# Routing tokens to tiles of one expert each, in place of computing every expert for every token

## The chip, the cores and the metric

The kernel runs on 1 core of one Trainium2 chip. The metric is the device time of one execution in microseconds (us); three runs of the kernel before gave a median of 170.99 us.

## The reference, cut to what matters

Eight batches of 128 tokens with 256 features go through a cross attention and then through a mixture of eight experts. The part that the change touches is the second:

```python
x = x + cross_attention(layernorm(x), ctx)
xf = layernorm(x).reshape(1024, 256)
probs = softmax(xf @ (gate_weight + 2 * gate_lora_B @ gate_lora_A).T)      # 8 experts
w, selected = top_k(probs, 2);  w = w / w.sum(-1)
gates, h = split(xf @ (gate_up[e] + 2 * lora), 2)                          # every expert e: 256 -> 2 x 128
out[e] = (silu(gates) * h) @ (down[e] + 2 * lora)                          # 128 -> 256
x = x + sum over the two selected experts of w * out[e]
```

## The kernel before, in words

P is 128 partitions, H 256 features, E 8 experts, I 128 hidden features, NT 8 batches. Each engine has its program written out by hand, with named counting semaphores between them, so each engine does its work in exactly the written order.

**Attention.** The loop over b in range(NT) (PE from L1123, ACT L448, DVE L709, POOL L298, SP L212) does for each batch the scores in both layouts (L908 for the maximum, L915 for the exponential), the row maximum on DVE (`max_chunk`, L593), its way to SBUF by a small DMA of SP (`load_max`, L205), the exponential on ACT (L391), the causal mask on POOL (`mask_chunk`, L295), the product with the values (`values`, L1024), the division (`softmax_divide`, L608 and L610), the output projection (`out_proj`, L998, by `products`, L798), the residual (L615), and the statistics of the second norm (L539, L540; `normaliser` on POOL, L253 to L259; `x2_normalise` on ACT, L420). `x2_T` (L1005) turns a normalised batch into features by tokens. In the same loop the low-rank parts of the expert weights are merged into `up_w` and `dn_w` (`lora_products`, `merge`, L586).

**Experts.** The merged weights are split into a high and a low fp32r part: the high part by ACT (`merge_high`), the low part by POOL (`merge_lows`, L286). Activations are split in the same way (`x2T_high`, `x2T_low`, `h_high`, `h_low`). The tokens form two groups of 512 (g = 0 and 1), and each of the 16 steps n (a group and an expert) computes one expert for all 512 tokens of a group: `gate_step` and `up_step` (six matmuls of 512 columns each, L798), silu on ACT (L410), `gate` on DVE (L664), the multiplication by the token's routing weight, zero where the expert wasn't chosen (`weigh`, L671), and `down_step` (12 matmuls of 256 columns, L1087), which sums over the experts in PSUM. Router logits are six matmuls of 512 columns per group; `route_choose` ranks them on DVE (L633 to L639). The weights reach all partitions over DRAM: SP writes them (L218) and loads eight broadcast copies of 256 KB per group (L226). `add_residual` (L654) adds the sum to `x_sb`, and SP stores two batches at a time (L231).

**Order around the change.** PE does `gate_step(0)` between the last attention block and `values(NT - 1)`; the last pieces of the attention are woven into the first expert steps. Four PSUM banks hold gate and up products of two steps, so PE works up to four steps ahead of `down_step`.

Of the kernel before, what the change touches and what calls it, by code (L numbers as in the profile page):

```python
# [12 lines left out]
def cross_attention_moe_kernel(nc, x, ctx_kv, Wq, Wkv, Wout, gate_w, gate_A, gate_B,  # L13
# [13 lines left out]
    NG = NT // GT  # L27
    GN = GT * P
# [12 lines left out]
    EXPERTS = (0, 4, 1, 5, 2, 6, 3, 7)  # L41
    HIGHS = (0, 4, 1, 5, 2, 3, 6, 8, 9, 7, 10, 11)
    HIGHS_AT = ((), (0,), (4, 1), (5,), (2,), (3,), (6,), (8,))
    LOWS_AT = (0, 1, 2, 1, 1, 1, 1, 1)
    UP_LOWS = (2, 2, 4, 4, 7, 7, 10, 10)
    DOWN_LOWS = (8, 8, 9, 9, 11, 11, 12, 12)

    ctx = ExitStack()
    with ctx:
# [18 lines left out]
        wr_hi = sb("wr_hi", [P, HC, P], F32R)  # L68
        wr_lo = sb("wr_lo", [P, HC, P], F32R)
# [7 lines left out]
        up_hi = sb("up_hi", [P, HC, E, 2 * I], F32R)  # L77
        dn_hi = sb("dn_hi", [P, E, H], F32R)
        up_lo = sb("up_lo", [P, HC, E, 2 * I], F32R)
        dn_lo = sb("dn_lo", [P, E, H], F32R)  # L80
        probsT = sb("probsT", [P, 2, NH, P])
        weight_all = probsT[:, :, :, :].rearrange("p k h n -> p (k h n)").rearrange("p (e n) -> p e n", e=E)
# [20 lines left out]
        x2hat = sb("x2hat", [P, H])  # L103
        lgT = sb("lgT", [E, GN])
        lg = sb("lg", [P, GT, E])
        lmax = sb("lmax", [P, GT])
        above = sb("above", [P, GT, E, E])
        equal = sb("equal", [P, GT, E, E])
        earlier = sb("earlier", [P, E, E])
        rank = sb("rank", [P, GT, E])  # L110
        chosen = sb("chosen", [P, GT, E])
        lsub = sb("lsub", [P, GT, E])
        lexp = sb("lexp", [P, GT, E])
        lpick = sb("lpick", [P, GT, E])
# [13 lines left out]
        xT_hi = sb("xT_hi", [P, HC, NT * P], F32R)  # L128
        xT_lo = sb("xT_lo", [P, HC, NT * P], F32R)
# [7 lines left out]
        silu = sb("silu", [P, 2, GN])  # L137
        gated = sb("gated", [P, 2, GN])
        h_f = sb("h_f", [P, 2, GN])
        h_hi = sb("h_hi", [P, 2, GN], F32R)  # L140
        h_lo = sb("h_lo", [P, 2, GN], F32R)
        rest_of_qk = sb("rest_of_qk", [P, 6 * GN])

        w_dram = nc.dram_tensor("weights", (NG, E, GN), F32, kind="Internal").ap()

# [9 lines left out]
        M_BANK = lambda b: bank[6][0:NH, PN:PN + P]  # L155
        X2_BANK = lambda t: bank[0 if t == GT - 1 else 5][:, 0:HC * P].rearrange("p (a n) -> p a n", a=HC)

# [11 lines left out]
        weight_loaded = [sem(f"weight_loaded{e}") for e in range(E)]  # L169
# [7 lines left out]
        xT_src = lambda g: slice(g * GN, (g + 1) * GN)  # L177
# [11 lines left out]
        def _(sp):  # L189
# [24 lines left out]

            for g in range(NG):

                sp.wait_ge(S_("wT_copied"), g + 1)
                sp.dma_start(w_dram[g], wT[:, g, :]).then_inc(S_("w_written"), 16)  # L218
                sp.wait_ge(S_("w_written"), 16 * (g + 1))
                for i in range(E):  # L220
                    if g == 0:
                        sp.wait_ge(S_("pv_done"), NT - 1 if i < E // 2 else NT)
                    else:
                        sp.wait_ge(S_("h_ready"), i + 1)
                    e = EXPERTS[i]
                    sp.dma_start(weight_all[:, i, :], w_dram[g, e:e + 1, :].to_broadcast([P, GN])).then_inc(weight_loaded[i], 16)  # L226
# [9 lines left out]
        def _(pool):  # L236
# [61 lines left out]
            for b in range(NT):  # L298
# [4 lines left out]
                if b >= 3 and b != GT + 2:  # L303
                    normaliser(1, b - 3, b - 2, "mv2_ready", b - 2)
# [941 lines left out]
```

## Time and profile before

| | |
|---|---|
| median of 3 runs (170.72 to 171.06) | 170.99 us |
| profiled execution: its own time, its span | 170.58 us, 168.8 us |
| PE busy | 153.3 us, 91% of the span |
| DVE, ACT, POOL busy | 105.4, 80.1, 53.5 us |
| chain that ended last: PE, DVE, DMA, ACT, issue | 65%, 14%, 8%, 5%, 5% |
| bytes moved by DMA | 11.18 MB |

The span runs from the first to the last instruction; the execution's own time holds 1.8 us more around it. "Busy" is the time in which an engine has an instruction under way; PE's matmuls overlap, so the duration of one is longer than the distance from one to the next, and what PE can do in a stretch is read from the distances. An fp32 matmul shows as two records. The chain follows back from the last instruction to what released each wait.

### The profile page before, as it was taken

The page shows a single profiled execution, that of the slowest core. Times are in us where ns is not written, and L with a number is a line of the kernel's source. Part 1 is how long each engine was busy: PE and PEld are TensorE (multiplying, and loading weights), DVE is VectorE, ACT ScalarE, POOL GpSimd, SP SyncE. Part 2 cuts the span into 40 slices and gives each one's busy share as a digit, 9 for nine tenths or more (in the row PEclk, how much of TensorE's full clock was granted, in tenths as well). Part 3 has the DMA queues.
Part 4 walks back from the last instruction along what each step waited for, and adds up shares of the span by engine and source line. Part 5 has one row for each costly group of instructions (what it writes and reads, how often), then busy time and mean ns, then how long its engine had stood idle before and what let it go on. Part 6 is the DMA issues. An engine that isn't in the chain of part 4 may idle for free.

```text
span 168.8 us, 3777 instructions
## 1 busy us (share of the span) xinstructions
PE 153.3 (91%) x1481; PEld 118.9 (70%) x1481; DVE 105.4 (62%) x224; ACT 80.1 (47%) x161; POOL 53.5 (32%) x93
## 2 busy tenths in 40 slices
PE   0597999999999999999999997999969989999972
PEld 0365676677777677778778876887758868888961
DVE  2778986859657657835498456555943466444463
ACT  1373557356657776586754617422653022222420
POOL 4276002256378657776740243330000000000000
PEclk9999999999999999999999999999999999999999
DMA  5999940000000000000000185000000594000003
GB/s 148 292 255 229 282 126 2 6 6 0 8 0 8 0 6 2 4 2 4 0 0 4 37 257 209 0 4 0 2 0 4 144 344 137 0 0 0 4 0 124
DMA packets 13042, 11.18 MB, mean 66 GB/s; under 512 B 6457, under 2 KB 10449, under 8 KB 13025
## 3 DMA queue, kind: packets, MB, share of 16 engines
q1 hardware_dynamic: 9584, 7.14, 15.7%
q0 software_dynamic: 544, 2.10, 4.6%
q10 hardware_dynamic: 2896, 1.70, 3.9%
q8 instruction: 12, 0.20, 0.5%
q14 instruction: 6, 0.04, 0.1%
HBM read 9.79 MB, written 1.08 MB: 64 GB/s over the span
## 4 chain that ended last, share of the span: by engine, by line
PE 65%; DVE 14%; DMA 8%; ACT 5%; issue 5%; POOL 1%; DVEq 0%; ACTq 0%
PE bank L798 29%; PE bank L1087 9%; PE bank L908 8%; DMA probsT<-weights 4%; PE bank L894 4%; PE bank L1024 4%; PE bank L915 3%; DVE m_sb L593 2%; DVE h_f L671 2%; DMA x_sb<-in_x 2%; DMA weights<-wT 2%; DVE xhat L552 2%; PE bank L973 2%; ACT silu L410 1%; DVE stats L539 1%
## 5 line engine op out<-in xcount | busy, mean ns | idle before, releaser
L798 PE MATMUL bank<-xT_hi,up_hi 128*128 128x512 f32 x64 | 27.1, 424 | 3.0 <-ACT silu L410 3.0
L318 ACT ACTIVATE h_hi<-h_f 128x512 fp32r<-128x512 f32 x16 | 10.1, 632 | 37.2 <-PE bank L1087 25.9
L295 POOL TENSOR_SCALAR_AFFINE_SELECT probsT<-probsT 128x512 f32<-128x512 f32 x32 | 19.7, 635 | 22.5 <-ACT probsT L391 22.5
L593 DVE TENSOR_REDUCE m_sb<-bank 128x4 f32<-128x512 f32 x32 | 20.4, 685 | 9.4 <-PE bank L908 9.4
L391 ACT ACTIVATE probsT<-bank 128x512 f32<-128x512 f32 x32 | 17.9, 590 | 17.3 <-PE bank L915 17.3
L798 PE MATMUL bank<-xT_hi,up_lo 128*128 128x512 f32 x64 | 25.3, 395 | 0.0
L798 PE MATMUL bank<-xT_lo,up_hi 128*128 128x512 f32 x64 | 25.3, 395 | 0.0
L676 DVE TENSOR_TENSOR h_lo<-h_f,h_hi 128x512 fp32r<-128x512 f32 x16 | 11.4, 713 | 21.0 <-ACT h_hi L318 21.0
L1087 PE MATMUL bank<-dn_hi,h_hi 128*128 128x256 f32 x64 | 18.4, 288 | 1.1 <-DVE h_lo L676 1.0
L915 PE MATMUL bank<-q_f,k_f 32*128 32x128 f32 x256 | 18.6, 283 | 0.0
L798 PEld LDWEIGHTS bank<-xT_hi,up_hi 128*128 128x128 f32 x64 | 12.0, 188 | 8.6 <-ACT silu L410 6.9
L1087 PE MATMUL bank<-dn_hi,h_lo 128*128 128x256 f32 x64 | 17.9, 279 | 0.0
L1087 PE MATMUL bank<-dn_lo,h_hi 128*128 128x256 f32 x64 | 17.8, 279 | 0.0
L908 PEld LDWEIGHTS bank<-k_f,q_f 32*128 32x128 f32 x256 | 13.6, 186 | 5.5 <-issue 5.0
L908 PE MATMUL bank<-k_f,q_f 32*128 32x128 f32 x256 | 16.3, 283 | 0.0
L915 PEld LDWEIGHTS bank<-q_f,k_f 32*128 32x128 f32 x256 | 15.5, 186 | 0.7 <-issue 0.7
L671 DVE TENSOR_TENSOR h_f<-probsT,gated 128x512 f32<-128x512 f32 x16 | 12.0, 748 | 5.1 <-DMA probsT<-weights 4.7
L798 PEld LDWEIGHTS bank<-xT_hi,up_lo 128*128 128x128 f32 x64 | 12.0, 188 | 2.9
L1087 PEld LDWEIGHTS bank<-dn_hi,h_hi 128*128 128x128 f32 x64 | 12.0, 187 | 2.1 <-DVE h_lo L676 1.5
L286 POOL TENSOR_TENSOR up_lo<-up_w,up_hi 128x512 fp32r<-128x512 f32 x8 | 10.3, 1291 | 9.8 <-ACT up_hi L318 9.8
L798 PEld LDWEIGHTS bank<-xT_lo,up_hi 128*128 128x128 f32 x64 | 12.1, 188 | 1.7
L1087 PEld LDWEIGHTS bank<-dn_lo,h_hi 128*128 128x128 f32 x64 | 12.0, 188 | 0.4
(137 smaller groups left out, 284.4 us busy)
## 6 DMA issues: line engine op xcount, KB each, us to landing
probsT<-weights SPq DMA_DIRECT2D x16, 256.0 KB, 5.5
x_sb<-in_x SPq DMA_DIRECT2D x4, 256.0 KB, 4.8
up_w<-in_L_ffn_gate_up_proj ACTq DMA_DIRECT2D x1, 1024.0 KB, 10.4
up_w<-in_L_ffn_gate_up_proj POOLq DMA_DIRECT2D x1, 1024.0 KB, 7.2
dn_w<-in_L_ffn_down_proj POOLq DMA_DIRECT2D x1, 1024.0 KB, 9.3
out<-x_sb SPq DMA_DIRECT2D x4, 256.0 KB, 2.2
ctx_sb<-in_ctx ACTq DMA_DIRECT2D x2, 128.0 KB, 5.6
wq_raw<-in_L_xattn_Wq ACTq DMA_DIRECT2D x1, 256.0 KB, 5.8
```

The costliest lines, as they stand in the source:

```text
L286: pool.tensor_tensor(merge_slice(up_lo, dn_lo, n), merge_slice(up_w, dn_w, n), merge_slice(up_hi, dn_hi, n).bitcast(F32), ALU.subtract).th ...
L295: pool.affine_select(out=ch, in_=ch, compare_op=ALU.is_ge, fill=0.0, base=0, pattern=[[0, 4], [1, P]], channel_multiplier=-1).then_inc(S_( ...
L318: act.activation(out_, in_, ACT.Copy, scale=scale).then_inc(S_(done), 1)
L391: act.activation(probsT[:, b % 2, 4 * j:4 * j + 4, :].rearrange("p h n -> p (h n)"), bank[2 + j % 2][:, :], ACT.Exp).then_inc(S_("exp_done ...
L593: dve.reduce_max(m_sb[:, b % 2, :].rearrange("p (u j t) -> p j u t", u=2, t=2)[:, c], S_BANK(b, c)[:, :].rearrange("p (u t n) -> p u t n", ...
L671: dve.tensor_tensor(h_f[:, k, :], weight_all[:, n % E, :], gated[:, k, :], ALU.mult).then_inc(S_("h_ready"), 1)
L676: dve.tensor_tensor(h_lo[:, k, :], h_f[:, k, :], h_hi[:, k, :].bitcast(F32), ALU.subtract)\
L798: last = pe.matmul(out_, a, m, start=start and i == 0, stop=stop and i == len(pairs) - 1, **kw)
L894: pe.matmul(S_BANK(s, j)[:, :], ident_b[:, :], causal[:, :, :].rearrange("p h n -> p (h n)"), start=True, stop=True, skip_group_check=True)
L908: last = pe.matmul(S_BANK(s, j)[:, c * P:(c + 1) * P], q_f[rows, c, tokens(s)], k_f[rows, c, tokens(s)], start=False, stop=True, skip_grou ...
L915: last = pe.matmul(bank[2 + j % 2][:, c * P:(c + 1) * P], k_f[rows, c, tokens(t)], q_f[rows, c, tokens(t)], start=True, stop=True)
L1087: last = pe.matmul(bank[6 + t // 2][:, (t % 2) * H:(t % 2 + 1) * H], a[:, k, tok], w[:, e, :], start=i == 0 and t % 2 == 0 and m == 0, sto ...
```

## The change

The expert part is rebuilt. The tokens form two groups of batches: batches 0 to 2 and 3 to 7. For every token DVE ranks the logits; a position for each (token, expert) chosen is counted by small matmuls with a triangle of ones; a token's row is written twice by indirect DMA of POOL to the rows of its two experts in a DRAM tensor that ACT has filled with zeros; SP loads tiles of 128 rows, each of one expert, at a row number read from a register. There are 13 tiles in the first group and 17 in the second, whatever the routing: the number that the worst case can need. For each tile PE transposes the rows, multiplies them in fp32 by the expert's weights, whose column PE reads into a register, transposes the hidden tile, and multiplies it by the down weights. The results of the first group are stored by SP to the same rows and gathered per token by indirect DMA of POOL; those of the second group are scattered by POOL to one row per (token, choice) and loaded back by SP. DVE adds the two rows of a token with their weights (`add_pair`). The split into high and low parts is gone.

```diff
+    ROUTED = ((0, 1, 2), (3, 4), (5, 6), (7,))
+    GROUP = (range(0, 3), range(3, NT))
+    ROWS = [len(g) * P for g in GROUP]
+    TILES = [(2 * n + E * (P - 1)) // P for n in ROWS]
+    SPARE = (7, 1)
+    XW = 272
+        xs = [nc.dram_tensor(f"xs{g}", (E * ROWS[g] + SPARE[g] * P, (H, XW)[g]), F32, kind="Internal").ap() for g in range(2)]
...
@@ SP
+            def load_tiles(g):
+                sp.wait_ge(S_("tiles_mapped"), g + 1)
+                sp.wait_ge(S_(f"x_scattered{g}"), 16 * 2 * len(GROUP[g]))
...
+                for i in range(TILES[g]):
+                    row = sp.value_load(row_x[g][0:1, i:i + 1], min_val=0, max_val=E * ROWS[g] + (SPARE[g] - 1) * P)
+                    sp.dma_start(xt[:, n, 0:(H, XW)[g]], xs[g][bass.ds(row, P), :]).then_inc(tile_loaded[n], 16)
...
+            load_tiles(0)
+            store_tiles(0, 5)
+            load_tiles(1)
+            store_tiles(5, TILES[0])
+            for b in GROUP[0]:
+                store_out(b)
+            sp.wait_ge(S_("y_scattered"), 16 * TILES[1])
...
+            for b in GROUP[1]:
+                sp.dma_start(yg[:, :, b, :], ys1[TILES[1] * P:, :].rearrange("(k j p) c -> j p k c", k=2, p=P)[j])\
+            for b in GROUP[1]:
+                store_out(b)
@@ POOL
+                if b == NT - 1:
+                    scatter_rows(0)
                 mask_chunk(b, 2)
                 mask_chunk(b, 3)
...
+            scatter_rows(1)
+            normaliser(1, 5, 6, "mv2_ready", 6)
+            scatter_rows(2)
+            normaliser(1, 6, 7, "mv2_ready", 7)
+            normaliser(1, 7, 8, "mv2_ready", 8)
+            for t in GROUP[1]:
+                scatter_rows(t)
+            for i in range(TILES[1]):
+                scatter_tile(TILE0[1] + i)
+                if 1 <= i < 4:
+                    gather_back(i - 1)
@@ ACT
+                if b == 0:
+                    fill(0, 0, E * len(GROUP[0]) + SPARE[0])
+                if b in (2, 4):
+                    half = E * len(GROUP[1]) // 2
+                    fill(1, *((0, half) if b == 2 else (half, 2 * half + 1)))
...
+            for s in range(NTILE):
...
+                    x_copy(s + 2)
+                    silu_step(s + 1)
+                    x2_again(4 + s)
+                    y_copy(s - 1)
+            y_copy(NTILE - 1)
+            exp_logits(3, NT, 2)
@@ DVE
                 if b == NT - 1:
-                    x2T_low(GT - 1)
+                    choose(0)
+                    slots(0)
+                    map_tiles(0)
                     residual(GT)
                     second_stats(GT)
...
+            for s in range(NTILE):
+                hT_copy(s)
+                    row_of_y(s)
+                    gate(s + 1)
+                if s == 0:
+                    choose(2)
+                if s == 1:
+                    slots(2)
+                if s == 3:
+                    choose(3)
+                if s == 4:
+                    slots(3)
+                    map_tiles(1)
...
+                if TILE0[1] + 5 <= s < TILE0[1] + 8:
+                    add_pair(s - TILE0[1] - 5)
+            pair_weights(3, NT, 2, len(ROUTED))
+            for b in GROUP[1]:
+                add_pair(b)
@@ PE
                 if b == NT - 1:
-                    router_logits(0, bank[1])
+                    positions(0)
...
+                if b == GT + 2:
+                    logits(0)
...
-            gate_step(0)
+            o_T_(NT - 2)
+            x2_T(4)
             values(NT - 1)
+            out_proj(NT - 2)
+            logits(1)
+            on_T(NT - 1)
+            tile_T(0)
+            x2_T(5)
             o_T_(NT - 1)
+            positions(1)
+            tile_T(1)
+            gate_up(0)
             out_proj(NT - 1)
+            x2_T(6)
+            for s in range(NTILE):
...
+                    tile_T(s + 2)
+                    gate_up(s + 1)
+                hidden_T(s)
+                    down_step(s - 1)
+                if last_of_group:
+                    down_step(s)
+                    tile_T(s + 1)
+                    tile_T(s + 2)
+                    gate_up(s + 1)
+            down_step(NTILE - 1)
```

The new functions that this calls, cut in the same way:

```python
def choose(r): # DVE: copy, is_gt, is_equal, mult, reduce_sum, is_lt, then one add per batch: 9 ops for ROUTED[0]
def slots(r): # DVE: mult, reduce_max, reduce_sum, subtract, minus one: 5 ops
def map_tiles(g): # DVE, on one partition: 12 ops
def pair_weights(lo, hi, nth, r): # DVE: 8 ops
def gate(n): h_f = bank[2 + n % 2][:, I:2 * I] * silu          # 128 x 128
def hT_copy(n): hT = bank[4][:, 0:P]                           # 128 x 128
def add_pair(b): two scalar_tensor_tensor of 128 x 256
def scatter_rows(t): # POOL: two indirect_dma_start of 128 rows
def gather_back(b): # POOL: two indirect_dma_start of 128 rows; the first waits for y_stored of all 13 tiles
def scatter_tile(n): # POOL: one indirect_dma_start of 128 rows
def logits(r): two matmuls x2T[:, t, ic, :], wr[:, ic, :] for each batch # 8 columns
def positions(r): two bf16 matmuls of 8 columns for each batch, one more at a group's end
def tile_T(n): two transposes of 128 x 128
def gate_up(n): value_load of the column; two fp32 matmuls 128 x 128 by 256 columns
def hidden_T(n): one transpose of 128 x 128
def down_step(n): one fp32 matmul 128 x 128 by 256 columns
def fill(g, lo, hi): act.dma_start(xs[g] rows lo * P to hi * P, zeros)
```

## Rows read from the trace of the kernel before

**Rows 1.** Stretches: start:end, length, busy PE PEld DVE ACT POOL, clock, DMA share, GB/s.

```profile
24.00:86.00 62.00, 61.08 (x927) 45.66 (x924) 41.81 (x95) 39.96 (x89) 35.86 (x57) 1.00 0.01 3
...
106.00:166.00 60.00, 56.34 (x327) 46.53 (x325) 32.94 (x57) 19.54 (x33) 2.58 (x2) 1.00 0.14 45
166.00:168.80 2.80, 0.00 (x0) 0.00 (x0) 0.22 (x1) 0.00 (x0) 0.00 (x0) 0.87 0.56 187
```

**Rows 2.** Chain that ended last: start us, us, what.

```profile
26.96 1.97 PE bank L798 x8
...
66.13 0.22 PE bank L984 x2
...
95.34 3.55 DMA probsT<-weights
...
142.33 1.41 PE bank L1087 x12
143.74 2.93 PE bank L798 x12
...
165.53 0.69 DVE x_sb L654
```

**Rows 3.** PE timeline around the last attention block: start us, us, then the operation.

```profile
76.72 1.16 PE L915 MATMUL bank<-q_f,k_f 32*128 32x128 f32 x16
```

**Rows 4.** DVE timeline, same stretch.

```profile
76.90 0.42 DVE L610 TENSOR_TENSOR o_nat<-bank,r_den 128x256 f32<-128x256 f32 x1
...
77.58 0.41 DVE L615 TENSOR_TENSOR x_sb<-bank,x_sb 128x256 f32<-128x256 f32 x1
78.03 0.43 DVE L539 BATCH_NORM_STATS2 stats<-x_sb 128x6 f32<-128x256 f32 x1
78.49 0.18 DVE L540 BATCH_NORM_AGGREGATE mv<-stats 128x2 f32<-128x6 f32 x1
```

**Rows 5.** POOL timeline, same stretch.

```profile
79.03 1.23 POOL L295 TENSOR_SCALAR_AFFINE_SELECT probsT<-probsT 128x512 f32<-128x512 f32 x2
80.34 0.22 POOL L253 TENSOR_SCALAR var_eps<-mv 128x1 f32<-128x1 f32 x1
80.64 0.56 POOL L254 TENSOR_TENSOR rstd<-var_eps,minus_half 128x1 f32<-128x1 f32 x1
81.30 0.27 POOL L259 TENSOR_SCALAR shift<-mv,rstd 128x1 f32<-128x1 f32 x1
...
86.07 0.30 POOL L253 TENSOR_SCALAR var_eps<-mv 128x1 f32<-128x1 f32 x1 [1.10 <-DVE mv L540]
86.45 0.73 POOL L254 TENSOR_TENSOR rstd<-var_eps,minus_half 128x1 f32<-128x1 f32 x1
87.29 0.51 POOL L259 TENSOR_SCALAR shift<-mv,rstd 128x1 f32<-128x1 f32 x1
```

**Rows 6.** Groups by line and form: busy us, mean ns, idle before.

```profile
L318 ACT ACTIVATE xT_hi<-bank 128x256 fp32r<-128x256 f32 x8 | 3.0, 380 | 3.0 <-PE bank L1005 3.0
...
L270 POOL DMA_DIRECT2D up_w<-in_L_ffn_gate_up_proj x1 | 1.1, 1110 | 0.0
...
L634 DVE TENSOR_TENSOR equal<-lg 128x256 f32<-128x256 f32 x2 | 0.9, 426 | 0.1
...
L624 DVE COPY lg<-bank 128x32 f32<-128x32 f32 x2 | 0.4, 192 | 4.3 <-PE bank L1036 4.3
```

**Rows 7.** ACT queue, issue of a 1 MB load.

```profile
2.94 0.54 ACTq L324 DMA_DIRECT2D up_w<-in_L_ffn_gate_up_proj  x1
```

**Rows 8.** SP queue, issue times.

```profile
4.35 3.81 SPq L194 DMA_DIRECT2D upB<-in_L_ffn_gup_lora_B  x1
...
95.34 4.38 SPq L226 DMA_DIRECT2D probsT<-weights  x8
```

**Rows 9.** DMA issues of the page: KB each, us from issue to landing.

```profile
probsT<-weights SPq DMA_DIRECT2D x16, 256.0 KB, 5.5
...
out<-x_sb SPq DMA_DIRECT2D x4, 256.0 KB, 2.2
```

More of the change, by code:

```diff
@@ new lines, in cross_attention_moe_kernel @@
+        full = [sb(f"full{g}", [1, E, len(GROUP[g])]) for g in range(2)]
+        iota_tile = sb("iota_tile", [1, max(TILES)], I32)
+        tile_no = sb("tile_no", [1, max(TILES)])
+        tile_row = sb("tile_row", [1, max(TILES)])
+        over = [sb(f"over{g}", [1, E, len(GROUP[g])]) for g in range(2)]
+        n_tiles = sb("n_tiles", [1, E])
+        part = sb("part", [1, E, E])
+        end = sb("end", [1, E])
+        skip = sb("skip", [1, E])
+        done = [sb(f"done{g}", [1, TILES[g], E]) for g in range(2)]
@@ L168, in cross_attention_moe_kernel @@
         m_loaded = [sem(f"m_loaded{i}") for i in range(2)]
[L169 removed]
+        tile_loaded = [sem(f"tile_loaded{n}") for n in range(NTILE)]
+        y_back = [sem(f"y_back{b}") for b in range(NT)]
         made = {}
@@ new lines, in positions @@
+            def positions(r):
+                pe.wait_ge(S_("chosen_ready"), r + 1)
+                if r == 0:
+                    pe.wait_ge(S_("router_consts"), 11)
+                for t in ROUTED[r]:
+                    g = group_of(t)
+                    j = t - GROUP[g][0]
+                    closes = t == GROUP[g][-1]
+                    products(slot_at(t), [(tri[:, :], chosen[:, t, :]), (ones[:, :], ahead[g][:, j, :])],
+                             "pos_ready" if t == ROUTED[r][-1] and not closes else None)
+                    if closes:
+                        products(count_at(g), [(ones[:, 0:1], ahead[g][:, j + 1, :])], "pos_ready")
@@ new lines, in tile_T @@
+            def tile_T(n):
+                pe.wait_ge(tile_loaded[n], 16)
+                if n == 0:
+                    pe.wait_ge(S_("x2T_copied"), GT)
+                elif n == TILE0[1] + 1:
+                    pe.wait_ge(S_("x1_ready"), NT)
+                elif n < TILE0[1] + 1:
+                    pe.wait_ge(S_("xt_copied"), n)
+                else:
+                    pe.wait_ge(S_("xt_copied"), n - 1)
+                for ic in range(HC):
+                    last = pe.transpose(XT_BANK(n)[:, ic, :], xt[:, n, ic * P:(ic + 1) * P], ident[:, :])
+                last.then_inc(S_("xt_T"), 1)
```

656 lines of the change are left out of this document (336 added, 320 removed).

## The prediction

> **What bounds the kernel now.** I read the stretches first. From 24 to 86 us (attention) PE is busy 61.08 of 62 us, from 106 to 166 us (the expert steps) 56.34 of 60, both at the full granted clock [rows 1]: PE sets the time in both, and only one real hole lies between them, where the broadcast weights come from DRAM, 3.55 us on the chain [rows 2]. Then the chain: an expert step is 2.93 us of gate and up products and 1.41 us of down products, 4.34 together [rows 2], so 16 steps are 69.4 us of PE. After the last matmul only two additions of 0.69 us [rows 2] and a store that lands 2.2 us after its issue [rows 9] are left, 168.8 us in all. The sum below is made on this clock; the execution's own time is 1.8 us more, 170.58, and that is 0.4 under the median of 170.99. The measurement can tell about 0.2% (0.3 us) from no change.
>
> **Expert work on PE: 69.4 us becomes 54.** Four fp32 matmuls of 128x128 by 256 columns take 1.97 us as eight records [rows 2], so 0.49 each. Two 128x128 transposes take 0.22 [rows 2], so 0.11 each. A tile has three such matmuls and three transposes: 1.47 + 0.33 = 1.80 us, and 30 tiles are 54.0. The routed tiles hold a quarter of the pairs and some padding, but such an fp32 matmul costs 0.49 against 1.41 / 12 = 0.12 for the same shape in fp32r [rows 2], so only 15 us are won. Steps overlap well in the written order: hidden_T(s) stands behind tile_T(s+2) and gate_up(s+1), 1.2 us, and what it waits for (a silu and a product of 128 columns, each under the 0.38 of a 256-column copy [rows 6]) is shorter. ACT has three operations of at most 0.38 per step, DVE two, so neither bounds. The two fp32r splittings go; they lay beside PE and give nothing by themselves.
>
> **The start of the first tile: a serial chain that the kernel before doesn't have.** Before, PE goes from attention straight into an expert step. Now a chain through DVE, POOL, DRAM and SP stands there.
> - logits(0), 12 records in block 6. Their distance isn't shown for 8 columns; bounds are nearly 0 and the 0.245 of a 256-column record; I take a transpose's 0.11, so 1.3 us. Block 7 then starts at 76.72 + 1.3 = 78.0 [rows 3].
> - DVE's division of block 5, before at 76.90 [rows 4], is done at about 78.5. choose(0) is nine operations between 0.19 (32 columns) and 0.43 (256 columns) [rows 6]: 2.5 us, to 81.0. PE's positions(0) waits for it, some 0.8 us. slots(0), five of 0.19, and map_tiles(0), twelve of 0.19 to 0.25 on one partition, follow: 3.7 us, to 84.7.
> - Residual(4) and its statistics, moved behind these, take 0.41 + 0.43 + 0.18 [rows 4]: 85.8. PE's out_proj(5) waits for this residual, and POOL's normaliser for the statistics: 0.22 + 0.56 + 0.27 [rows 5], to 86.9.
> - On POOL the first scatters stand behind this normaliser. An indirect issue isn't in the trace. Nearest are POOL's plain DMA issue, 1.11 us [rows 6], and as ends 0.2 (its smallest operation [rows 5]) and 3.81 (an issue of SP with many small pieces, on a full queue [rows 8]). I take 1.1. Two scatters, two masks (1.23 [rows 5]), two scatters, a normaliser (1.05), two scatters: 8.9 us, to 95.8. values(7) waits for the masks; PE has little else and idles for most of 88 to 101.
> - The rows land about 1.8 us later (2.2 less the issue of 0.4 [rows 9]), SP reads a register, issues (0.4) and the tile lands 2.2 after that: about 100.8.
> - PE then has tile_T(0), x2_T(5), o_T_(7), tile_T(1), gate_up(0), out_proj(7) and x2_T(6) with their copies: the loop begins at 104.2, where before steps 0 to 3 had their products nearly done.
>
> **The loop.** 54.0 less the two tile_T and the gate_up(0) already done (1.4) is 52.6. Beside the tiles PE has x2_T(7), logits and positions of five batches: 2.3. DVE's slots(3) and map_tiles(1), 4 us in one go before the next hT_copy, exceed its slack of about 2: 2.0. The group boundary, where down_step(12) waits for its copy and gate_up(13) for tile 13's: 1.1. A register read by PE before each gate_up isn't in the trace: below it is 0, since it may run while the products queued before it are at work; above, 0.54, a whole DMA issue of ACT [rows 7]. I take 0.1, near the low end, since 0.7 us of queued work lies ahead of it: 3.0. The Trainium skill ("DMA: Bandwidth & Descriptors", Latency and other measured facts) gives a floor of about 600 ns for such a load; all of it exposed would make this term 18 us. No row here shows one.
> The second group's loads start after slots(3), near 114, and the last scatters: about 119.5, and its first tile is wanted at 135, so they are hidden.
>
> **The fill.** ACT issues zeros for 31 and 41 blocks of 128 rows: 4.1 and 5.7 MB of writes, near 33, 47 and 61 us, where DMA moves 3 GB/s [rows 1]. Eight loads of 256 KB issued from 95.34 in 4.38 us [rows 8] with 5.5 us to landing [rows 9] make about 0.3 MB/us, so the writes end long before 95. What they can meet are the small loads of the maxima, and ACT's queue: an issue for four times the rows of the 1 MB load (0.54 [rows 7]) is some 2 us; with a full queue, as SP's 3.81 [rows 8], more. I take 1.0 on the path (0 to 13, the latter the whole first fill).
>
> **The tail.** After the last down_step: y_copy 0.5, indirect issue 1.1 and landing 1.8, five SP loads of 256 KB, the last issued 1.7 later and landing 5.5 after that, less overlap, 6.6 with the wait; add_pair of two 0.43 operations 0.9; store 2.2 and a hand-over: 13.2. pair_weights(3..7) is some 4 us and lies beside it. Before, this was 3.4.
>
> **Sum:** 104.2 + 1.0 + 52.6 + 2.3 + 2.0 + 1.1 + 3.0 + 13.2 = 179.4, plus 1.8 is 181.2. I forecast 181 us, 6% slower. Its own range, from terms other than the rivals', is 175 to 188.
>
> **A: faster.** Everything is dear because I priced each hand-over singly. If an indirect issue is 0.6 us, the chain is 3 us shorter (tile 0 at 98); with fill, register reads and DVE's hold all covered (6.0), and five loads at 0.3 MB/us from the first byte (tail 10.5): 181.2 - 3.0 - 6.0 - 2.7 = 169.5. For it speaks that 15 us of PE work truly go and that the lookahead is two tiles; against it that all must come at once, since the start chain is of DVE operations whose prices are shown. It decides if tile 0 is transposed before 98 and a step is 1.80. Chance 0.13; about level, 170.9: 0.02.
>
> **B: POOL becomes the bound.** In rows, the same three normaliser operations take 0.22, 0.56, 0.27 alone and 0.30, 0.73, 0.51 at 86 us [rows 5], beside DVE's comparisons: POOL is slowed by DVE, by half. In the second group POOL has 17 scatters and 6 gathers against 17 steps of 1.9 us; it decides from 32 / 23 = 1.4 us an issue. At 1.8 the start is 4 us later and POOL ends 41 us after the group's first tile (140 + 41 = 181), then the rest of the tail: about 195. The Trainium skill ("SBUF — State Buffer", Who interferes with whom) says that VectorE and GpSimd share a port pair under an exclusive lock, so the later of the two fully blocks, and that a GpSimd DMA can't write its descriptors while DVE is in a two-port mode. By that rule, the slowed rows agree. Chance 0.20.
>
> **C: SP's queue holds DVE.** SP does 17 loads, then 8 stores of first-group tiles, and only then may POOL gather; add_pair(0), in step 18, stands before the next hT_copy on DVE. With 0.75 us for register and issue, stores end near 140, in time. From 1.0 us on they are late; at 1.3 they land at 154, the gather at 158, and DVE waits 10 us from 147: 192. Against: the eight issues of 4.38 us are 0.55 each [rows 8], and the register read must then be dear. Chance 0.12.
>
> **D: the fill blocks ACT** for the length of a queue that is full (3.81 [rows 8]) or more, and exponentials wait: +8, 189. Chance 0.08.
>
> That leaves 0.45 for the forecast; slower altogether is 0.45 + 0.20 + 0.12 + 0.08 = 0.85. The range reaches from 168 (A and a little more) to 199 (B).
>
> **What would show it.** In the profile after: fp32 matmul records 0.245 us apart and steps of 1.9 us; PE idle from about 88 to 101, released by the DMA into xt; POOL's indirect issues near 1.1 us (B: 1.4 or more, and POOL on the chain at the end); SP's loads 0.75 apart (C: DVE's scalar_tensor_tensor released by DMA yg in the middle of group 1); ACT's fill issue near 2 us (D: above 4). In the hole PE may also lose its full clock, as it does after its last work (0.87 in the last 2.8 us [rows 1]): first tiles at the lower level would add up to 3 us. The prediction is wrong if the hole is under 5 us or the last tile ends before 155.

## The result, and the profile after

The kernel after takes 214.55 us (median of 4 runs, 212.0 to 218.45), the kernel before 171.03 beside it: ratio 1.2426, 95% interval 1.2351 to 1.2501. The medians and spreads given are over all executions of a kernel, but in kernels with the change some executions are slow ones, over 1.5% longer than the fastest, and every ratio, and every difference between kernels below, leaves these out (the kernel after is then 212.6). The forecast was 181 us with a range of 168 to 199. The sign was right (slower), the size was not: 41.5 us lost instead of 10, and no case of the range reached that far. The profiled execution took 212.0 us with a span of 210.2, so 30.8 us more than the span of 179.4 that the sum gave.

First the stretches of the kernel after, to hold against [rows 1]: start:end, length, busy PE PEld DVE ACT POOL, clock, DMA share, GB/s.

```profile
24.00:80.00 56.00, 52.98 (x797) 38.96 (x796) 34.85 (x73) 31.09 (x70) 22.50 (x42) 0.97 0.54 178
80.00:92.00 12.00, 10.42 (x94) 7.90 (x94) 8.24 (x33) 3.37 (x7) 1.65 (x4) 0.64 0.01 1
92.00:108.00 16.00, 7.75 (x59) 5.33 (x57) 5.92 (x21) 3.06 (x7) 10.29 (x16) 0.71 0.15 58
108.00:118.00 10.00, 7.33 (x29) 5.23 (x29) 2.17 (x10) 5.08 (x11) 1.30 (x4) 0.69 0.39 112
118.00:136.00 18.00, 13.98 (x77) 10.50 (x77) 10.37 (x51) 7.16 (x23) 9.70 (x10) 1.00 0.41 142
140.00:160.00 20.00, 18.41 (x92) 14.12 (x93) 5.69 (x27) 9.72 (x32) 1.94 (x2) 1.00 0.46 133
160.00:172.00 12.00, 2.38 (x13) 1.64 (x11) 0.43 (x1) 1.49 (x6) 3.83 (x4) 0.72 0.30 98
172.00:176.00 4.00, 2.90 (x9) 2.33 (x9) 1.49 (x6) 0.77 (x2) 3.08 (x4) 0.50 0.41 131
...
200.00:210.20 10.20, 0.00 (x0) 0.00 (x0) 4.94 (x12) 0.00 (x0) 0.00 (x0) 0.50 0.60 193
```

Three things differ from before. Attention moves 178 GB/s instead of 3 and PE is busy 95% of it, not 98.5%. The clock, at 1.00 before to the end of the experts, is 0.64 to 0.71 from 80 to 118 (and already 0.50 from 74 to 76). From 160 to 172 PE does almost nothing, and behind its last product, which ends at 196.6, stand 13.6 us where [rows 1] has 2.8.

The chain shows what ended last (start us, us, what); [rows 2] is its counterpart:

```profile
34.54 5.90 DMA q_f<-mT
...
66.39 5.63 DMA q_f<-mT
...
102.77 2.39 DMA xs<-xrow,index
106.21 2.04 DMA xt<-xs
...
164.70 1.69 DMA xs<-y_sb
168.62 2.85 DMA probsT<-xs,index
...
197.81 2.42 DMA ys<-y_sb,y_row
201.18 3.98 DMA probsT<-ys
```

Every hand-over through DRAM is on it, and two of the small loads of the maxima, 5.90 and 5.63 us long. PE's timeline names the waits in its brackets:

```profile
72.07 1.16 PE L1040 MATMUL bank<-q_f,k_f 32*128 32x128 f32 x16 [1.44 <-DMA q_f<-mT]
...
86.63 0.18 PE L923 MATMUL bank<-chosen,tri 128*128 128x8 bf16 x1 [1.39 <-DVE ahead L729]
...
108.29 0.69 PE L1197 MATMUL bank<-ident,xt 128*128 128x128 f32 x2 [5.60 <-DMA xt<-xs]
...
161.27 1.11 PE L923 MATMUL bank<-up_w,xh 128*128 x4
173.10 0.47 PE L1223 MATMUL bank<-ident,h_f 128*128 128x128 f32 x1 [10.72 <-DVE h_f L800]
...
174.70 1.91 PE L923 MATMUL bank<-up_w,xh 128*128 x4
177.08 0.48 PE L1223 MATMUL bank<-ident,h_f 128*128 128x128 f32 x1 [0.46 <-DVE h_f L800]
```

The wait of 10.72 us is released by DVE's gate. What DVE itself had waited for, and what POOL, stands in their timelines:

```profile
171.57 0.48 DVE L791 SCALAR_TENSOR_TENSOR x_sb<-probsT,wts,x_sb 128x256 f32<-128x256 f32 x1 [11.83 <-DMA probsT<-xs,index]
...
175.51 0.48 DVE L791 SCALAR_TENSOR_TENSOR x_sb<-probsT,wts,x_sb 128x256 f32<-128x256 f32 x1 [2.46 <-DMA probsT<-xs,index]
...
167.25 1.06 POOL L368 DMA_INDIRECT probsT<-xs,index  x1 [10.73 <-DMA xs<-y_sb]
```

And SP's queue, which POOL's gather waits for (start, length of the whole group, count):

```profile
106.21 14.99 SPq L254 DMA_DIRECT2D xt<-xs  x13
124.12 9.72 SPq L260 DMA_DIRECT2D xs<-y_sb  x5
137.20 18.72 SPq L254 DMA_DIRECT2D xt<-xs  x17
156.86 8.18 SPq L260 DMA_DIRECT2D xs<-y_sb  x8
```

This is rival C, complete: 17 loads of 1.1 us each, then 8 stores, the last at 165.0; POOL's gather at 167.25; DVE's sum of tile 0 at 171.57, with the next hT_copy behind it; PE stands. The forecast had these loads begin at 119.5; they began at 137.20, behind the last scatters (133.97, landing 2.44 later). When PE resumes, the clock is 0.50 and the four records of gate and up take 1.91 us instead of 1.11. But the clock doesn't pace the next two steps. They take 4.0 us each (hidden_T at 173.10, 177.08 and 181.12), because the gate that each waits for stands on DVE behind the sum of tile 1 (175.51) and that of tile 2 (179.59). These wait for POOL's next gathers, which come 4.0 us apart, two gathers and a scatter at a time. Kernels 2 and 4 show the same two steps of 4.0 us. They are still rival C.

### The profile page after: what moved, and what is told of

Read it like the earlier page. It is cut to its first block, busy times and chain, and to the rows that moved or that the text cites. A ratio compares the mean times of both kernels' runs of the same rounds, so it can differ in the third digit from the quotient of the medians.

```text
span 210.2 us, 4464 instructions
## 1 busy us (share of the span) xinstructions
PE 153.8 (73%) x1389; PEld 111.9 (53%) x1389; DVE 101.1 (48%) x324; ACT 83.2 (40%) x207; POOL 80.9 (38%) x141
## 3 DMA queue, kind: packets, MB, share of 16 engines
q0 software_dynamic: 2416, 7.29, 10.4%
## 4 chain that ended last, share of the span: by engine, by line
PE 35%; DMA 15%; issue 15%; DVE 12%; SPq 11%; POOL 8%; ACT 1%; POOLq 0%; DVEq 0%; ACTq 0%
PE bank L923 14%; PE bank L1033 6%; DMA q_f<-mT 5%; SPq L252 4%; SPq L254 4%; PE bank L1019 3%; POOL ys L375 3%; POOL xs L360 3%; PE bank L1156 2%; DMA xs<-xrow,index 2%; DMA probsT<-ys 2%; SPq L259 2%; PE bank L1040 2%; POOL rstd L302 2%; PE bank L1197 1%
## 5 line engine op out<-in xcount | busy, mean ns | idle before, releaser
L923 PE MATMUL bank<-up_w,xh 128*128 x120 | 34.5, 412 | 2.1 <-issue 1.0
L375 POOL DMA_INDIRECT ys<-y_sb,y_row x17 | 16.8, 987 | 28.6 <-ACT y_sb L415 21.8
L923 PEld LDWEIGHTS bank<-up_w,xh 128*128 128x128 f32 x120 | 21.7, 201 | 7.2 <-issue 5.0
L415 ACT ACTIVATE y_sb<-bank 128x256 f32<-128x256 f32 x30 | 11.5, 384 | 28.1 <-issue 14.6
L923 PE MATMUL bank<-dn_w,hT 128*128 x60 | 19.6, 410 | 2.6 <-ACT y_sb L415 2.0
L1223 PE MATMUL bank<-ident,h_f 128*128 128x128 f32 x30 | 9.1, 302 | 16.5 <-DVE h_f L800 14.5
L813 DVE COPY hT<-bank 128x128 f32<-128x128 f32 x30 | 8.7, 290 | 25.2 <-PE bank L1223 19.5
L360 POOL DMA_INDIRECT xs<-xrow,index x16 | 16.1, 1009 | 10.0 <-issue 4.3
L1040 PEld LDWEIGHTS bank<-q_f,k_f 32*128 32x128 f32 x256 | 16.7, 198 | 2.7 <-DMA q_f<-mT 1.7
L1197 PE MATMUL bank<-ident,xt 128*128 128x128 f32 x60 | 12.4, 295 | 6.9 <-DMA xt<-xs 5.6
L1033 PEld LDWEIGHTS bank<-k_f,q_f 32*128 32x128 f32 x256 | 13.6, 186 | 6.7 <-issue 4.9
L415 ACT ACTIVATE xh<-bank 128x256 f32<-128x256 f32 x30 | 11.3, 380 | 7.0 <-PE bank L1197 6.4
## 6 DMA issues: line engine op xcount, KB each, us to landing
xs<-blank ACTq DMA_DIRECT2D x1, 3968.0 KB, 14.7
xs<-blank ACTq DMA_DIRECT2D x1, 2856.0 KB, 11.2
xs<-blank ACTq DMA_DIRECT2D x1, 2720.0 KB, 11.2
```

The costliest lines, as they stand in the source:

```text
L360: pool.indirect_dma_start(xs[g], bass.IndirectOffsetOnAxis(ap=index[:, k, t:t + 1], axis=0), row, None, bounds_check=E * ROWS[g] - 1).then ...
L375: pool.indirect_dma_start(ys1, bass.IndirectOffsetOnAxis(ap=y_row[:, i:i + 1], axis=0), y_sb[:, n, :], None, bounds_check=TILES[1] * P + 2 ...
L415: act.activation(out_, in_, ACT.Copy, scale=scale).then_inc(S_(done), 1)
L813: dve.tensor_copy(hT[:, n % 2, :], bank[4][:, 0:P]).then_inc(S_("hT_copied"), 1)
L923: last = pe.matmul(out_, a, m, start=start and i == 0, stop=stop and i == len(pairs) - 1, **kw)
L1033: last = pe.matmul(S_BANK(s, j)[:, c * P:(c + 1) * P], q_f[rows, c, tokens(s)], k_f[rows, c, tokens(s)], start=False, stop=True, skip_grou ...
```

## The experiments

All ratios are to the kernel before, measured beside each.

**1. The sums out of the loop.** The gathers of group 0 go behind scatters 13 to 15, the sums behind the loop.

```
-                if 1 <= i < 4:
-                    gather_back(i - 1)
+                if 13 <= i < 16:
+                    gather_back(i - 13)
...
-                if TILE0[1] + 5 <= s < TILE0[1] + 8:
-                    add_pair(s - TILE0[1] - 5)
+            for b in GROUP[0]:
+                add_pair(b)
```

> The kernel after, with POOL's gathers of the first group behind the scatters of tiles 26 to 28 and DVE's add_pair(0) to add_pair(2) behind the loop. Theory C (SP's queue holds DVE, and DVE holds PE): the hole of 10.7 us in PE from 162.4 to 173.1, released by DVE's h_f, goes, and so do the steps at the lower clock behind it (two steps in 8 us against 1.65 each): 199 to 203 us. Rival, POOL's queue is what bounds the second group: its issues (1.3 us with the gap) come in the same number, so the time stays within 3 us of 214. Rival, the register loads pace PE: 212 to 216.

205.25 us (200.17 to 208.78, 4 runs). The fastest run is 12.4 less than the kernel after, and one run gives no ratio (the medians of all runs differ by 9.3). The hole is gone; a stretch of this kernel:

```profile
166.00:176.00 10.00, 10.00 (x52) 7.89 (x51) 3.35 (x18) 5.15 (x17) 5.69 (x6) 1.00 0.23 80
```

PE's last product ends at 179.9 instead of 196.6, 16.7 us earlier, and the span is 202.2 instead of 210.2: only 8.0 of these reach the end. POOL's last scatter and SP's queue tell why:

```profile
188.93 1.03 POOL L375 DMA_INDIRECT ys<-y_sb,y_row  x1 [0.30 <-issue]
...
183.56 8.36 SPq L264 DMA_DIRECT2D out<-x_sb  x3
192.02 2.46 SPq L276 DMA_DIRECT2D probsT<-ys  x5
```

The loads of y leave 12.1 us after PE's last product ends. Most of that is POOL's: its six gathers now stand between the last scatters, at 1.3 us each, and the last scatter leaves 9.0 us behind the product. Scatters land some 2.4 us after their issue (197.81 in the chain above), so the loads of y, which wait for all of them, could leave at about 191.3 at the earliest; the order on SP adds 0.7. With C's hole gone, POOL's queue holds the end, as rival B had it. Experiments 6 to 9 take this up.

**2. The fill in seven pieces**, one behind exp_chunk(b, 1) of each block, instead of three large ones.

```
+                if b < NT - 1:
+                    fill(*FILLS[b])
...
+            FILLS = ((0, 0, 10), (0, 10, 20), (0, 20, 31), (1, 0, 10), (1, 10, 20), (1, 20, 30), (1, 30, 41))
```

> The kernel after, with the zero fill issued in seven pieces of 10 or 11 blocks of rows, one per attention block, right behind the copy of the maxima. Theory D (the fill delays the small loads of the maxima, which PE waits for): landings of 5.9 and 5.6 us at 34.5 and 66.4 fall to about 2 to 3, attention ends 5 to 7 us sooner. If the granted clock of 0.64 to 0.79 from 72 to 118 us comes from the hole that this wait makes, it goes too, 5 to 8 us more: 200 to 204 us. Rival, the low clock has its cause in the chain between attention and tiles: only 207 to 210 us. Rival, it is the number of bytes that counts and not their order: no change, 214.

205.57 us (203.17 to 207.88, 4 runs), 9.1 less. The gain is near the second figure expected, but the landings aren't: the two small loads on the chain still take 4.98 and 4.53 us, not 2 to 3. PE's wait for the maxima in block 6 is 0.33 us instead of 1.44, block 7 starts at 78.65 instead of 82.82, the load of tile 0 at 101.76 instead of 106.21. PE's last product ends 8.7 us earlier, so about half of the gain arises only inside the loop of tiles (the first six steps take 15.8 us instead of 18.2, the hole is 8.59); why isn't shown.

**3. Both.**

> The fill in seven pieces and the late gathers and additions together. If C and D are separate causes, their gains add: 186 to 192 us. If one of them only moves into the other's slack, not below 197.

199.8 us, ratio 1.1634 (1.1552 to 1.1715). 12.8 less than after, where the two alone gave 12.4 (one run) and 9.1: far from additive, since the end no longer follows PE (the last scatter leaves at 184.68, 9.1 us behind the last product). The clock still falls, now only at 78 us: PE waits 0.34 us for the maxima here (1.44 in the kernel after), so it wasn't that wait alone. Nor does that wait always lower it: kernel 1 is the kernel after up to that point and waits 1.43 us, and its clock stays at 1.00 from 74 to 78 us, where the profile of the kernel after reads 0.68.

**4. Stores to constant rows.** The 13 stores of group 0 go to row n * P, not to the row in the table: part of the rows read back are others. Only the register read goes.

```
-                    row = sp.value_load(row_x[0][0:1, n:n + 1], min_val=0, max_val=...)
-                    sp.dma_start(xs[0][bass.ds(row, P), :], y_sb[:, n, :])
+                    row = n * P
+                    sp.dma_start(xs[0][row:row + P, :], y_sb[:, n, :])
```

> The kernel after, but SP stores the 13 tiles of the first group to constant rows: the register load goes from the stores, not from the loads, and the outputs of batches 0 to 2 are gathered from rows that may not hold their results. Theory C: the eight stores behind the 17 loads come 0.4 to 0.5 us apart in place of 1.10, POOL's first gather and DVE's first addition 4 to 5 us sooner: 208 to 211 us, and the distance of the stores gives a register load as 0.6 to 0.7 us. Rival, SP is paced by the DMA issue itself: distance 1.1 stays, 214.

204.24 us, ratio 1.1829 (1.1731 to 1.1927), 8.7 less than the kernel after, more than the 4 to 7 expected.

```profile
154.60 4.11 SPq L260 DMA_DIRECT2D xs<-y_sb  x8
```

8 stores in 4.11 us instead of 8.18: 0.5 us each instead of 1.1 (the span runs from the first issue's start to the last one's end). A register read on SP from SBUF therefore costs 0.5 to 0.6 us. PE's wait shrinks from 10.72 to 5.29 us, and POOL's first gather leaves at 160.95 instead of 167.25. The prediction's price for register and issue together was 0.75, with 1.0 as the point from which C decides.

**5. Work that keeps PE busy.** On kernel 3, 38 matmuls nobody reads.

```
+            def keep_busy(n):
+                for _ in range(n):
+                    pe.matmul(bank[0][:, :], ident_b[:, :], causal[:, :, :].rearrange("p h n -> p (h n)"),
+                              start=True, stop=True, skip_group_check=True)
```

> Kernel e3_both with 38 matmuls added that compute nothing anyone reads (bf16, 128x512, into PSUM bank 0 while it is free): 6 behind the logits of tiles 0 to 2, 8 in block 7 behind the weight products, 24 between the last transposes of attention and the transposes of tile 0. Theory 1: the clock of 0.50 that e3_both shows from 79 to 115 us comes from what TensorE does there (first 12 products of 8 columns, then waits), not from the DMA traffic or the time. Then the granted clock stays at 1.00 or near it to the start of the loop; the work of block 7 and the boundary (about 15 us at half the clock, of which about half is given back, less what is waited for anyway, and less 38 x 0.2 us of added work) ends 3 to 5 us earlier: 195 to 197 us against 199.8. Rival: the clock falls for a reason outside TensorE's own work (the fill's traffic, a limit that follows on the busy first 75 us): then it stays at 0.50 whatever is added, and the added work costs time at half the clock: 200 to 206 us.

201.3 us (198.76 to 201.85, 6 runs), ratio 1.1713 (1.1657 to 1.1769): no gain. Timeline and stretches of this kernel:

```profile
76.54 1.50 PE L922 MATMUL bank<-wr,x2T 128*128 128x8 f32 x12
78.12 1.83 PE L1265 MATMUL bank<-causal,ident_b 128*128 128x512 bf16 x5
...
102.13 6.81 PE L1265 MATMUL bank<-causal,ident_b 128*128 128x512 bf16 x23
```

```profile
78.00:82.00 4.00, 3.93 (x13) 2.56 (x12) 0.00 (x1) 0.00 (x0) 0.00 (x0) 0.58 0.10 28
82.00:86.00 4.00, 2.65 (x53) 2.08 (x51) 3.32 (x11) 1.63 (x3) 1.22 (x2) 1.00 0.00 0
...
102.00:106.00 4.00, 3.95 (x12) 1.45 (x12) 3.42 (x13) 0.00 (x0) 2.12 (x4) 0.57 0.17 68
106.00:110.00 4.00, 3.39 (x18) 1.66 (x16) 0.00 (x0) 0.66 (x2) 0.00 (x0) 1.00 0.34 99
```

The clock falls while the first wide matmuls run, behind the narrow logits, and is back at 1.00 behind them, where kernel 3 stays at 0.50 from 80 to 90. That return alone shows nothing, for kernel 8, with the same attention and none of the added products, has it too:

```profile
78.00:82.00 4.00, 4.00 (x27) 3.24 (x26) 1.82 (x7) 0.00 (x0) 0.00 (x0) 0.57 0.02 6
82.00:86.00 4.00, 3.00 (x65) 2.51 (x65) 3.17 (x14) 2.33 (x6) 1.23 (x2) 1.00 0.00 0
```

What speaks for the theory is the mean clock over all runs, 0.907 to 0.927 here and 0.913 to 0.920 in kernel 7 against 0.855 to 0.893 in kernel 3 and 0.854 to 0.888 in kernel 8, and the stretch ahead of the loop, 1.00 from 106 to 110 where kernels 3 and 8 read 0.50. So TensorE's own work does move the clock. The price was wrong. From the transpose of tile 0 to the loop PE takes 4.59 us (108.78 to 113.37) instead of kernel 3's 6.80 (106.15 to 112.95), and the clock gives back 2.2 us. But tile 0 is transposed 2.63 us later: its load leaves at 105.59 instead of 104.02, and the added products, in part at the lower level, still run when it lands.

**6. Another order of the queues.** SP loads 10 tiles of group 1, stores the 8 of group 0, loads the other 7; gathers behind scatters 9 and 12 and at the end.

```
+            load_tiles(1, 0, 10)
+            store_tiles(5, TILES[0])
+            load_tiles(1, 10, TILES[1])
...
+                if i == 9:
+                    gather_back(0, (0,))
+                if i == 12:
+                    gather_back(0, (1,))
+            gather_back(1)
+            gather_back(2)
```

> The fill in 7 pieces, as in e2_fill_pieces, and a new order of the queues around group 1: SP loads tiles 0 to 9 of group 1, then stores the 8 tiles left of group 0, then loads tiles 10 to 16; POOL reads one choice of tile 0 back behind scatter 9, the other behind scatter 12, and the 4 other gathers behind the last scatter; the sums of group 0 come behind the loop. No wait of the tile loop then depends on a store of group 0, and POOL's backlog at the end is gone (in e3_both the last three scatters went out at 176.68, 180.68 and 184.68, the last one 10 us behind TensorE's last product). Theory: the last scatter goes out 1 to 2 us behind the last product, and the time is 7 to 9 us less than e3_both's 199.8: 191 to 193 us. Rival: the loads of tiles 10 to 16, behind the stores, come late and make TensorE wait 3 to 6 us: 195 to 199 us.

199.52 us, ratio 1.1664 (1.1626 to 1.1701): nothing over kernel 3, a miss for both theories (191 to 193, 195 to 199). One execution of it, the profiled one, was disturbed (760.9 us), so its reading comes from the next.

**7. Both 5 and 6.**

> e6_order with the 38 added matmuls of e5_warm. If both act as their theories say, and each at its own place, the gains add: 187 to 190 us. If the clock stays low in spite of the added matmuls: 192 to 198 us.

200.68 us, ratio 1.1692 (1.1632 to 1.1753), a miss too. SP's queue:

```profile
177.81 10.84 SPq L264 DMA_DIRECT2D out<-x_sb  x3
188.76 2.46 SPq L277 DMA_DIRECT2D probsT<-ys  x5
```

The last scatter had left at 179.05, but the loads of y stand behind the stores of out tiles 0 to 2.

**8. The loads of y first** (on kernel 6): the loop of store_out(b) over group 0 moves behind the loads.

> e6_order (199.5 us), in which SP issues the 5 loads of group 1's results before the stores of tiles 0 to 2 of the output, no longer behind them. Theory: in e3_both and e7_order_warm the end was again an order on SP's queue: the stores of out tiles 0 to 2 wait for the sums, these for POOL's last gathers, and the loads of y stand behind them (188.76 in e7_order_warm, where the last scatter had left at 179.05 and takes 2.4 us). With the loads first they go out at 181.5 and the end comes 6 to 7 us earlier: 192 to 194 us. Rival: the gathers themselves, the last of which leaves at 184.34 and lands 2.86 us later, hold the sums as long: then 197 us or more.

200.99 us, ratio 1.1703 (1.1646 to 1.1760): the rival's case. The loads leave at 179.31, 9.4 us earlier than in kernel 7, and the end stays. On DVE:

```profile
184.26 0.48 DVE L793 SCALAR_TENSOR_TENSOR x_sb<-probsT,wts,x_sb 128x256 f32<-128x256 f32 x1 [8.64 <-DMA probsT<-xs,index]
...
187.66 0.48 DVE L793 SCALAR_TENSOR_TENSOR x_sb<-probsT,wts,x_sb 128x256 f32<-128x256 f32 x1 [2.39 <-DMA probsT<-xs,index]
```

Now the sums of tiles 1 and 2 wait for the gathers, and those of tiles 3 to 7 stand behind them. The same wait has moved from SP's queue to DVE's. The gathers themselves got slower: the last one leaves at 182.18, 2.2 us earlier than in kernel 7, and its rows are there only at 187.66, 5.5 us later, where kernel 7 took 2.9. In kernel 8 the five loads of y were in flight beside it, in kernel 7 not; that they are the reason isn't tested.

**9. The table of tiles later** (on kernel 8).

```
                     slots(0)
-                    map_tiles(0)
                     residual(GT)
                     second_stats(GT)
+                    map_tiles(0)
...
+                if b == NT - 1:
+                    scatter_rows(0)
                 if b >= 3 and b != GT + 2:
                     normaliser(1, b - 3, b - 2, "mv2_ready", b - 2)
-                if b == NT - 1:
-                    scatter_rows(0)
```

> e8_loads_first with two moves in block 7: VectorE builds the table of tiles (12 short instructions, 2.4 us) behind residual and statistics of tile 4 instead of ahead of them, and POOL scatters tile 0 ahead of the normaliser of tile 4 instead of behind it. Theory: the six scatters, which end the wait for tile 0, stand behind VectorE's queue and not behind the clock alone; they begin at 86 to 88 us instead of 91.2, the loop of tiles starts 3 to 4 us earlier, and so does the end. Rival: what holds the last scatter is the normalisers and masks between the scatters, or the wait for probsT that the scatters cause; then 0 to 1 us.

196.83 us, ratio 1.1429 (1.1373 to 1.1485), 4.3 less than kernel 8. POOL:

```profile
86.48 1.17 POOL L359 DMA_INDIRECT xs<-xrow,index  x1 [2.31 <-DVE index L748]
```

In kernel 8 the first of the six scatters left at 90.81 and the last at 100.22: the first gained 4.3 us and the last 2.9, the masks and normalisers between them took the rest. At the end of the two profiled executions 1.3 us of this are left (loads of y at 177.98 and 179.31, spans 196.1 and 197.2), so the rest of the 4.3 isn't accounted for.

**10. The kernel before with 12 narrow products** at the end of block 6.

```
+                    pe.wait_ge(S_("max_done"), NC * NT)
+                    for _ in range(12):
+                        pe.matmul(bank[1][:, 0:E], ident[:, :], ident[:, 0:E], start=True, stop=True, skip_group_check=True)
```

> The kernel before, with 12 added fp32 products of 8 columns (128x128 by 128x8, into the free bank 1, read by nobody) at the end of block 6, where the kernel after makes its logits. Theory: these narrow products and the low load on TensorE around them are what lowers the clock in the kernel after. Then the granted clock of before, 1.00 throughout, falls to 0.5 to 0.7 for some microseconds behind them and the time grows by 3 to 5 us over 171.0. Rival: only waits lower the clock; then it stays at 1.00 and the time grows by the products' own 1.3 to 1.6 us, or less.

175.58 us against 171.63: ratio 1.0242 (1.0200 to 1.0285), 4.0 us.

```profile
76.92 2.74 PE L1192 MATMUL bank<-ident 128*128 128x8 f32 x24
...
82.53 0.80 PE L798 MATMUL bank<-xT_hi,wr_hi 128*128 128x512 f32 x1
```

```profile
78.00:80.00 2.00, 2.00 (x19) 1.83 (x21) 0.00 (x0) 0.03 (x1) 0.00 (x0) 1.00 0.00 0
80.00:82.00 2.00, 2.00 (x44) 1.82 (x48) 1.36 (x4) 1.82 (x4) 1.04 (x1) 0.82 0.00 0
82.00:84.00 2.00, 2.00 (x16) 1.32 (x9) 0.00 (x0) 0.74 (x2) 1.83 (x5) 0.50 0.00 0
84.00:86.00 2.00, 2.00 (x20) 1.61 (x20) 0.00 (x0) 0.58 (x2) 0.62 (x2) 0.82 0.00 0
```

No wait, no fill, and a PE without a gap: the clock still falls, behind the narrow products, to 0.50 and is back at 1.00 from 86 us on, and a record of 512 columns takes 0.80 instead of 0.50. Of the 4.0 us about 2.6 are the products themselves (24 records; the logits of the kernel after, 12 records in 1.5 us, are half as many), so about 1.4 are the clock. That narrow products can lower it with no wait of PE is shown, for 24 records; the rival falls. It isn't shown that the 12 of the logits always do. In nine of the ten readable profiles with logits the clock fell within 3 us of their first record, but in that of kernel 2 it stayed:

```profile
75.60 1.50 PE L922 MATMUL bank<-wr,x2T 128*128 128x8 f32 x12
...
78.00:82.00 4.00, 2.81 (x55) 2.24 (x53) 3.18 (x11) 1.63 (x3) 1.22 (x2) 1.00 0.00 0
```

It fell there behind the next narrow products and a wait of 1.38 us, at 82 to 83.

**11. The sums in order of arrival** (on kernel 9): weights of group 1 first, then the sums and stores of tiles 0, 3 to 7, 1, 2.

```
+            for b in (0, 3, 4, 5, 6, 7, 1, 2):
+                add_pair(b)
```

> e9_map_later (196.8 us) with another order of the sums at the end: VectorE makes the weights of group 1 first, then the sum of tile 0, those of tiles 3 to 7, and those of tiles 1 and 2 last; SP stores the output in that order. Theory: in e8_loads_first the loads of y left at 179.31 instead of 188.76 and it brought nothing, because VectorE's sums of tiles 1 and 2 stood ahead of those of tiles 3 to 7 and waited for the last gathers to 184.26 and 187.66; with the order turned the five sums begin when y lands, near 183 to 184, and the last two find their rows there: 2 to 4 us less, 193 to 195 us. Rival: the 5 loads (1.3 MB at 256 GB/s) and the gathers share the DMA engines so that all of them land near 187 whatever the order: 196 us or more.

192.58 us (190.88 to 194.25, 6 runs), ratio 1.1178 (1.1122 to 1.1234), 4.8 less than kernel 9 and a little below the expectation. DVE:

```profile
180.52 0.48 DVE L793 SCALAR_TENSOR_TENSOR x_sb<-probsT,wts,x_sb 128x256 f32<-128x256 f32 x1 [2.52 <-DMA probsT<-ys]
```

The sums of tiles 3 to 7 begin at 180.52, and the last of all is made at 188.61.

This is the fastest version with the change: half of what it had cost (41.5 us) is gone, 20 remain, and the kernel before stays the better one.

## Why the prediction was wrong

Right in direction. Two terms failed: the 0.75 us for a register read and an issue on SP, which measured 1.1 and made rival C the fact, and the 1.0 us for the fill. The steps one by one:

- **"A tile is 1.80": too dear.** At the full clock six steps take 10.14 us (hidden_T at 150.36 and at 160.50), 1.69 each. The fp32 matmul is 0.43 to 0.44, not 0.49: the 1.97 us of four in [rows 2] hold the latency of the last. Without any wait the products make 0.87 + 0.43 + 3 x 0.11 = 1.63 us.
- **Register reads of PE, 3.0 us:** the 0.06 that is left per step is all that they can cost there, 0.1 was taken. The Trainium skill's floor of about 600 ns for such a read ("DMA: Bandwidth & Descriptors", Latency and other measured facts) would have made 18 us, had it been exposed on PE; these steps exclude that. On SP, where nothing hides it, experiment 4 gives 0.5 to 0.6 us, and there the page's figure was the one to use: with it a load is 0.5 + 0.6 = 1.1 us, and C decides from 1.0.
- **Block 7 starts at 78.0: measured 82.82.** Here the term of the fill was mis-sized and its mechanism wrong. ACT issues each fill in 0.39 us, not 2 and not 4, so D doesn't happen. The victims are the loads of maxima: two of them land only after 5.90 and 5.63 us, with writes of 14.7 and 11.2 us under way. The term stood at 1.0 us. Of the 4.8 measured, 1.9 are waits (block 6's first scores for the exponential start at 72.07, before at 70.16), and 2.9 are the low clock between there and block 7 (10.75 us, where kernel 2 takes 7.89 at 1.00). The low clock is in part luck of the profiled execution: kernel 1 runs the same code in 8.41. Cutting the fill in pieces brought 9.1 in all. The text named both victims and priced the wrong one.
- **choose, slots, map 6.2 us: 7.3** (83.14 to 90.4). The forecast named 0.8 us for positions(0) in between and didn't add it: the 3.7 are used up by the 17 operations. PE took 0.5 there. **Residual and statistics 1.1: 1.1. Indirect issue 1.1:** 0.97 to 1.17 and a gap of 0.30, so 1.3 on POOL; the chain of six took 10.4, not 8.9, and ACT's normalised row (0.64) had been left out. **Landing and load 5.0: 4.5.** Each link was within 1 to 2 us. Tile 0 was there at 108.25 instead of 100.8, and 4.8 of the 7.5 come from the late block 7.
- **The loop begins at 104.2: about 114.8.** The transposes and products between tile 0 and the loop took 6.5 us instead of 3.4, at half the clock; kernel 5 shows that the clock is 2.2 of these 3.1. The text had the low clock as an afterthought "in the hole", up to 3 us. It came earlier, from 73 us on, and not only from idling: narrow products can lower it without a wait (experiment 10). With the 2.9 in block 6 it cost about 5 us of the profiled execution ahead of the loop.
- **Rival C, chance 0.12, was the fact.** The condition was there in the text: 1.0 us for a load or store, and 1.1 was measured. What was wrong is the 0.75 taken for it. The text didn't keep to one price: the 5.0 us from the last scatter to tile 0 leave 0.6 for the same read (1.8 + 0.4 + 2.2 are 4.4), and C's 0.75 leaves 0.35. With 0.6 C's condition would have been met in the text. The price of C was wrong too: it stood at 11 us over the forecast, and the hole alone is 10.72, and the two steps behind it, held by the sums of tiles 1 and 2, took 8.0 instead of 3.4.
- **Rival B** took 1.4 us an issue as its point, from steps of 1.9 us. The steps are 1.69, so 17 of them are 28.7 us and the point for 23 issues is 1.25; 1.3 was measured. So its condition was met, if barely. It was hidden behind C, and in experiments 1 and 3, without C's hole, POOL's last scatter leaves 9 us behind PE's last product. Its order is what experiments 6 to 11 had to work around.
- **DVE's hold 2.0: 1.32; boundary 1.1: about 3.3** (144.9 to 148.25; two waits for ACT's copy of y, 0.18 and 0.66, one of 0.39 for its copy of xh, and products that nothing overlaps). **Tail 13.2: 13.6.**

Together, against the sum's 179.4: the loop begins 9.6 us later than the 105.2 it gave with the fill (block 7 4.8, the chain to tile 0 2.7, the half clock behind it 3.1, less the fill's 1.0). It lasts 81.8 us instead of 61.0: the hole 10.7, the two steps behind it 4.6, the boundary 2.2, and 3.3 more. These 3.3 are a net figure. The cheaper tiles, register reads and DVE's hold give back about 7, so some 10 us are lost in other places of the loop, most in its first steps (18.2 us for six, from hidden_T at 116.87 to 135.03, where six steady ones take 10.1) and 2.2 between 181 and 190; they weren't taken apart further. The tail is 0.4 longer. That is 30.8.

The range failed because it was built from one rival at a time. The fill's delay, C and the low clock don't exclude each other, and all three came. A range over cases that can happen together has to reach to their sum.

What of the 15 us saved on PE? They are really saved, and more: 30 tiles of 1.69 us are 51 us of PE against 69.4. But before, PE was the bound from 24 to 166 us. In kernel 11 its first tile is transposed at 102.53, behind a wait of 3.75 us, and its last product ends at 173.3, 18.0 us ahead of the end of the span. How far these two ends could be shortened beyond experiment 11 wasn't tried.

## What to carry to other kernels

Routing that saves matmuls pays only if what it adds isn't serial: here choose, scatter, load, gather and sum each wait for the last piece of the one before, and the ends cost more than the middle saves. When an engine's queue mixes work for two pipelines, write down for each entry what stands behind it and when its input really comes; in this kernel one wait was moved from DVE to SP's queue and back to DVE before it left the path. When one bound is lifted, ask what the next one is: here POOL's queue stood right behind SP's. Bulk writes that nobody waits for can delay the small loads that somebody does wait for; cut into pieces, each behind the copy of the maxima, they cost 9.1 us less here.

## What the runs showed of the hardware that was not expected

- Products of 8 columns lowered TensorE's granted clock although the profile shows no gap on the engine (experiment 10: 1.00, then 0.82, 0.50, 0.82 and 1.00 again in stretches of 2 us). The Trainium skill ("TensorE: Matmul & The Clock Gate", Part 1: The HAM clock gate) tells of a clock that follows how busy TensorE has been, with idle time as what lowers it; by the profile's busy time in this stretch, 2.00 of 2.00 us, it would have stayed up. But busy there means an instruction under way, and doesn't tell how much of the engine it uses.
- The same instructions don't always meet the same clock. Kernels 2 and 3 have the same attention and the same narrow logits near 76 us; from 78 to 82 us the clock reads 1.00 in one and 0.57 in the other.
- A load of 4 KB in the same DMA engines as a write of 2.7 to 4.0 MB took 5.6 to 5.9 us, and 4.5 to 5.0 beside pieces of 1.3 to 1.5 MB, with the issue of that write over in 0.39 us: the engine that issues a large DMA isn't the one that pays.
- An indirect DMA of 128 rows of about 1 KB costs POOL 0.97 to 1.17 us and 0.30 to the next, scatter or gather; a register read on SP 0.5 to 0.6 us, so that a load with a row from a register takes twice an ordinary issue. On PE, with products queued ahead, the same read is nearly free (at most 0.06 us a step).
